# Weight stores of the first block issued by GpSimd instead of SyncE, in an AdaLN + 4-bit FFN kernel

## What is computed

```
gate = relu(cond @ W3 + b3)
z    = relu(((64 * x + sum_over_sequence(x)) * gate) @ W2 + b2)
w_up   = ((codes_up   - 7.5) * repeat(scale_up, 64)).T   + lora_a_up   @ lora_b_up
w_down = ((codes_down - 7.5) * repeat(scale_down, 64)).T + lora_a_down @ lora_b_down
out  = x + relu(z @ w_up + b_up) @ w_down + b_down
```

## Time and profile before

| | |
|---|---|
| median of 3 runs | 747.97 us (747.75 to 749.12) |
| the profiled execution | 748.49 us |
| its span, first to last instruction | 746.7 us |
| TensorE matmuls | 3274, busy 740.1 us (99%) |
| VectorE, ScalarE, GpSimd busy | 553.8, 419.9, 79.5 us |
| granted TensorE clock | 0.999 over the span |
| DMA | 170.20 MB, mean 228 GB/s |
| `made` store | 16 of 1280 KB, median 5.6 us to landing |
| `plain` store | 16 of 512 KB, median 8.2 us to landing |

### The profile page before, as it was taken

How to read it: one execution, slowest core, us unless ns; L and a number is a source line. 1 busy time by engine, 2 the same in 40 slices (tenths; PEclk the granted TensorE clock), 3 DMA queues, 4 the chain that set the end, 5 groups by cost and what they waited for, 6 DMA issues and landing times. The chain is left out here.

```text
span 746.7 us, 9586 instructions
## 1 busy us (share of the span) xinstructions
PE 740.1 (99%) x3274; PEld 613.2 (82%) x3274; DVE 553.8 (74%) x727; ACT 419.9 (56%) x727; POOL 79.5 (11%) x69
## 2 busy tenths in 40 slices
PE   9999999999999999999999999999999999999998
PEld 8888878878888878888888888888888888888886
DVE  6997776768948488767767687767775877757596
ACT  5963474766562565758456275666646353534540
POOL 0065524243420000000000000000000000000000
PEclk9999999999999999999999999999999999999999
DMA  9959968778444996666407896666515696666563
GB/s 291 322 178 378 319 228 280 253 250 274 169 197 141 376 331 222 212 195 194 161 27 252 284 382 225 226 198 197 184 57 193 221 386 223 189 190 195 196 194 130
DMA packets 68946, 170.20 MB, mean 228 GB/s; under 512 B 7650, under 2 KB 8034, under 8 KB 66338
## 3 DMA queue, kind: packets, MB, share of 16 engines
q1 hardware_dynamic: 68034, 168.20, 66.7%
q10 hardware_dynamic: 864, 1.39, 0.6%
HBM read 129.71 MB, written 40.89 MB: 228 GB/s over the span
## 5 line engine op out<-in xcount | busy, mean ns | idle before, releaser
L1186 PE MATMUL ps<-x_hi,ring 128*128 128x512 f32 x672 | 262.0, 390 | 0.6 <-issue 0.4
L1188 PE MATMUL ps<-x_hi,ring 128*128 128x512 f32 x672 | 261.8, 390 | 0.0
L1187 PE MATMUL ps<-x_lo,ring 128*128 128x512 f32 x672 | 261.7, 389 | 0.0
L1186 PEld LDWEIGHTS ps<-x_hi,ring 128*128 128x128 f32 x672 | 126.2, 188 | 27.8 <-ACT ps L526 1.0
L1188 PEld LDWEIGHTS ps<-x_hi,ring 128*128 128x128 f32 x672 | 126.2, 188 | 26.3
L1187 PEld LDWEIGHTS ps<-x_lo,ring 128*128 128x128 f32 x672 | 126.2, 188 | 26.0
L409 ACT ACTIVATE xt<-xt,gated,gate_n 128x64 f32<-128x64 f32 x216 | 74.7, 432 | 36.5 <-DVE gated L779 36.5
L518 ACT ACTIVATE f<-ps,small_in 128x512 f32<-128x512 f32 x96 | 64.8, 690 | 42.3 <-PE ps L1188 42.3
L971 DVE TENSOR_TENSOR x_lo<-x_sum,x_hi 128x512 fp32r<-128x512 f32 (+1 forms) x96 | 76.7, 819 | 4.2 <-ACT x_hi L556 3.4
L892 DVE TENSOR_TENSOR ps<-s,ps 128x512 f32<-128x512 f32 x48 | 33.3, 693 | 50.2 <-PE ps L1188 49.8
L929 DVE TENSOR_TENSOR res<-ps,res 128x512 f32<-128x512 f32 x71 | 47.6, 687 | 20.1 <-PE ps L1188 19.7
(11 more groups left out here) (90 smaller groups left out, 1024.4 us busy)
## 6 DMA issues: line engine op xcount, KB each, us to landing
ring<-made_w SPq DMA_DIRECT2D x336, 256.0 KB, 3.9
made_w<-made SPq DMA_DIRECT2D x16, 1280.0 KB, 5.6
xt<-in_x SPq DMA_DIRECT2D x32, 256.0 KB, 7.8
code<-in_codes SPq DMA_DIRECT2D x16, 512.0 KB, 8.4
scale<-made_s SPq DMA_DIRECT2D x16, 512.0 KB, 7.8
made_w<-plain SPq DMA_DIRECT2D x16, 512.0 KB, 8.2
res<-in_x SPq DMA_DIRECT2D x4, 2048.0 KB, 10.5
out<-res SPq DMA_DIRECT2D x12, 512.0 KB, 5.7
```

Of the source, the lines that this page charges most:

```text
L1186: pe.matmul(dest, w_hi, a_hi, start=start, stop=False, skip_group_check=True)
L1187: pe.matmul(dest, w_hi, a_lo, start=False, stop=False, skip_group_check=True)
L1188: return pe.matmul(dest, w_lo, a_hi, start=False, stop=stop, skip_group_check=True)
```

## The change

Both store functions move from SyncE's block to GpSimd's. GpSimd issues store_plain(u) and store_made(u) behind its four sums of unit u, with the same waits (L307, L312) and the same semaphores. SyncE's loop keeps scales, codes, the residual and the x tiles; its waits behind the loop stay.

```diff
@@ SyncE
-            def store_plain(u):
-
-                sp.wait_ge(plain_split, u + 1)
-                sp.dma_start(made_w[uid(FIRST[u]), :, 5:7],
-                             plain[u % 2][:, A11:A22 + 1].rearrange("p v h c -> p v (h c)").bitcast(F32)).then_inc(plain_stored[u % 2], 16)
-
-            def store_made(u):
-                sp.wait_ge(made_split, u + 1)
-                sp.dma_start(made_w[uid(FIRST[u]), :, 0:5],
-                             made[:, u % 2].rearrange("p c h v -> p c (h v)").bitcast(F32)).then_inc(made_stored[u % 2], 16)
...
-                store_plain(u)
                 if 2 <= u < 10:
                     load_x(1, u - 2)
-                store_made(u)
@@ GpSimd
+            def store_plain(u):
+
+                pool.wait_ge(plain_split, u + 1)
+                pool.dma_start(made_w[uid(FIRST[u]), :, 5:7],
+                             plain[u % 2][:, A11:A22 + 1].rearrange("p v h c -> p v (h c)").bitcast(F32)).then_inc(plain_stored[u % 2], 16)
+
+            def store_made(u):
+                pool.wait_ge(made_split, u + 1)
+                pool.dma_start(made_w[uid(FIRST[u]), :, 0:5],
+                             made[:, u % 2].rearrange("p c h v -> p c (h v)").bitcast(F32)).then_inc(made_stored[u % 2], 16)
...
                 pool.tensor_tensor(to[:, 4], w[:, A12], w[:, A22], ALU.subtract).then_inc(made_summed, 1)
+                store_plain(u)
+                store_made(u)
```

## The result

The changed kernel takes 762.1 us, median of 5 runs (761.85 to 762.9), against 747.75 (747.46 to 749.12) for the kernel before in the same comparison: a ratio of 1.0191 (95% interval 1.0179 to 1.0202), 14.35 us slower. The forecast was 9.1 us slower; direction and range hold, the size was more than a third too small. The profiled execution took 762.1 us with a span of 760.3, 13.6 us more than the profiled execution before (748.49 and 746.7).

The account below looks back on a forecast made before the run. TensorE, 99% busy, was taken as the bound, with VectorE just late for it in units 5 to 10. 7.1 + 2.0 = 9.1 us on 748.49 gave 757.6, less 0.5 for the median: 757.1 us, range 749 to 767.

Parts of the forecast that it names:

- the x2p_lo pair of unit 10: VectorE's two x2p_lo instructions before TensorE's unit 10 wait, delayed by GpSimd sums among them: 1.6 us.
- TensorE's wait in unit 10 ends later: Sum of VectorE's delays in units 5 to 9 and the x2p_lo pair, less 3.3 us of credits: +7.1 us.
- end of the stretch: Units 14 and 15: late sums(15) delay made_low(15), stalling TensorE 0.6 us, then a bank freed 1.4 us late: +2.0 us.
- The bound: TensorE is busy 99%; VectorE is just late with x2p_lo, so its delays in units 5 to 10 cost TensorE fully.
- The issue on GpSimd: Each store's DMA issue on GpSimd was taken as 1.1 us, between 0.32 and 1.71 us seen on SyncE.
- Rival (d): Slow GpSimd issue of 2 to 3 us, sums past made_high's place: 4 to 12 us more, 761 to 770; chance 0.22.
- The wait: GpSimd must await made_split(u) before sums(u+1), so they begin 1.1 us behind made_low(u), when VectorE is busiest.
- The step that failed: GpSimd's sums and VectorE's SBUF instructions alternate, each waiting for one instruction; 2.6 us each in units 5, 6, 9, 10.
- the credits: Gate and made_low no longer stand beside GpSimd: 2.0 and 1.3 us back over eight units, 3.3 us taken off.
- unit 7, a D unit: Sums run mostly beside VectorE's PSUM work, plain_low at 2.4 instead of 2.3, gate about 5.7 instead of 5.4: 0.3 us.
- Unit 4: Begins like unit 7 but with x2p_lo in it, 0.7 us; its made_low credit pays, so it ends no later.
- Stores as waits: Plain stores land by about when plain_high(u+2) wants them, counted 0; landing in 8 us would cost 1 to 2 us per unit pair.

Follow-up runs that it names:

- the wait alone: Kernel before, all stores on SyncE, plus one ordering: GpSimd starts the sums of unit u only when made_split has reached u; 750.65 us, ratio 1.0034.
- the small DMA in front of the sums: Kernel before (stores on SyncE) plus the made_split wait and a 2 KB GpSimd transfer between that wait and the sums; 765.48 us, ratio 1.023.
- the run with memsets: Changed kernel with GpSimd's four sums per unit replaced by memsets of the same outputs, so its output is wrong; 744.76 us, ratio 0.9956.
- the filled wait: Changed kernel with 16 extra matmuls ahead of TensorE's x2p_lo waits in units 6 and 10; 760.63 us, ratio 1.0167.
- the gap run: Changed kernel with a 64-column memset and a wait for it on GpSimd between the made store and the next sums; 756.68 us, ratio 1.0114.
- The runs with other orders: Changed kernel with store_made(u-1) issued after unit u's sums: behind the plain store 787.08 us; ahead of it, with an explicit made_split wait before the sums, 762.68 us.

## Why the prediction was right in sign and short in size

The ledger of TensorE, before against after, in the prediction's order. The forecast's figure is set beside what the traces show.

| | forecast | measured |
|---|---|---|
| made_low(9) ends later (155.80 to 164.27), from units 4 to 9 | +5.5 | +8.5 |
| the x2p_lo pair of unit 10 | +1.6 | +2.9 |
| TensorE's wait in unit 10 ends later (158.34 to 169.74) | +7.1 | +11.4 |
| from there to unit 15 (225.22 to 238.31), the 1.2 GHz stretch in it | none | +1.7 |
| end of the stretch (241.54 to 255.71 on TensorE) | +2.0 | +1.1 |
| behind it, where an old gap near 268 is gone | none | -0.6 |
| span | +9.1 | +13.6 |

*The bound.* Right for units 5 to 10: what makes VectorE later there is paid in full. But the ledger of the prediction began too late. TensorE waited 1.0 us for x2p_lo in unit 2 already, and was 1.6 us behind its old times at the start of unit 4's second half (LoRA matmuls at 88.19, before 86.64), 0.3 of it from before that wait.

*The issue on GpSimd.* Taken at 1.1 us between 0.32 and 1.71; measured 0.53 for made and 0.58 for plain. The 3.5 us of sums are uninterrupted, so in units 4 to 11 made_high never waits for GpSimd. Rival (d) is out by its own sign: the issue is fast. Its 761 to 770 us came to pass for another reason.

*The wait.* The prediction read one row wrongly: the 7.11 us of the earlier trace rows are how long GpSimd had been idle, while made_low(6), whose store it waited for, had ended at 119.94, 5.75 us before 125.69. Nothing in the sum rests on it. The step itself was right, and the first half of the cause: L742 begins directly behind made_low(u-1) and the issue, in VectorE's busiest time, and is waited for by no DMA. Its price with turns taken is what the wait alone shows, 2.6 us.

*The step that failed* is "Each waits until the other's instruction is over", taken as alternation: "GpSimd's 1.29, 0.73, 0.73 and 0.73 go between them". The row at 194.34 showed GpSimd holding VectorE for one sum, and that was read as one turn. In the changed kernel GpSimd holds it for four. The terms, as far as made_low(9), each with the credits (the shorter gate and made_low) added back: unit 7, a D unit, was put at 0.3 and cost 1.8, since plain_low is held for the rest of the sums (3.01 us for 1.23); unit 8, put at 0.7, cost 1.0; units 5, 6 and 9, put at 2.6 each, cost 2.2, 2.9 and 2.2. Behind them the x2p_lo pair was held 2.9 us instead of 1.6. The cost of units 5, 6 and 9 was thus about right for a wrong reason, which is luck, and that of the D unit and of the pair was 2.8 us too small in all.

The Trainium skill (SBUF — State Buffer, SBUF: two separate sides) says that whichever instruction starts first, GpSimd's or one of VectorE with two SBUF inputs, gets the port pair for the whole instruction. The wait alone agrees, turn by turn; the changed kernel goes beyond it: four sums run one behind the other for 3.4 us and hold one instruction of VectorE for 3.0, and the small DMA in front of the sums shows what makes the difference. The Trainium skill (SBUF — State Buffer, Who interferes with whom) also says that a GpSimd instruction which only writes SBUF doesn't contend with a two-input VectorE instruction; the run with memsets agrees, with x2p_lo at 689 ns.

*The clock* was missing from the sum. Behind the waits of 3.7 us TensorE came back at 1.2 GHz; behind the single 0.79 us of the earlier trace rows it hadn't. It costs some 1.5 us here, by the ledger and by the filled wait. The length of a wait alone doesn't tell whether it comes: see the gap run, where one of two waits of 2.42 us had no slow stretch behind it.

*Credits.* The lengths were right, gate 167 ns and made_low 1493, but the count was not. The 3.3 us are those of eight units, 4 to 11, and were taken off the cost of units 5 to 9. There they come to 2.4 us: 0.85 and 0.81 of gate in units 5 and 8, and 0.25 of made_low in each of units 6, 7 and 9. So 0.9 us too much was taken off.

*Unit 4.* Put at nothing; its made_low ends 0.7 us later (96.73 for 96.05). VectorE waits there for x2p_hi (2.03 us), and ScalarE, which makes it, waits 1.6 and 1.4 us for tiles of TensorE. So this is the wait of unit 2 coming back, and not GpSimd's work in unit 4. With the 0.9 us of credits and the 1.5 and 0.3 us of units 7 and 8, less 0.4 in units 5, 6 and 9 together, this makes the 3.0 us by which the table's first row is off.

*End of the stretch.* Sized at 0.6 and 1.4 us, measured as stalls of about 0.2 and 0.9: made_high(15) does wait for the sums and made_low(15) does end late (234.5, put at 222.0 plus the shift of some 11.4 to 13), but the first of the two stalls came out 0.4 and the second 0.5 us smaller than forecast.

*Stores as waits.* Next to nothing in this order, as forecast: ScalarE has one wait of 6.6 us for a plain store in the whole stretch, near 72 us (before, three of 16.3 us in all), and TensorE has no wait between 70 and 96. The runs with other orders show how near that was.

What stays open is why an issue lets GpSimd keep the port. Shown is only that a DMA issue directly in front does it, with 2 KB as with 1280, that a memset in front doesn't, that the sums of unit 0 with nothing in front aren't kept together either, and that a short memset with a wait behind the issue undoes it. How the remaining 5.4 to 6 us between the gap run and the wait alone divide into start offset and clock wasn't separated.

## What to carry to other kernels

Before a DMA issue is moved to GpSimd, look at what its wait drags along in program order, and at what VectorE reads from SBUF at that moment; the issue itself was the cheapest part of this change (0.53 us, hidden). If GpSimd must both issue and compute, keep the issue away from the front of its SBUF-reading instructions, and start these where VectorE is idle: here that ordering, with all stores on SyncE, took the kernel 1.4 us below the one before. If two stores share a queue, look at which of them is waited for first. Of a longer stall on TensorE, allow also for matmuls at half the clock behind it; here that was 1.5 us of 14.

## What was not expected of the hardware

- With a DMA issue directly in front, four GpSimd instructions ran for 3.4 us without a break and held one VectorE instruction with two SBUF inputs for 3.0 us of it; without the issue each side had its turn. Two sizes, 2 KB and 1280 KB, gave the same.
- After some waits TensorE ran 7 to 13 matmuls of 512 columns at 0.43 us from start to start instead of 0.23, and the length of the last wait doesn't decide it. It happened behind both waits of 3.7 us in the changed kernel, behind one of two waits of 2.42 us in the gap run, and behind 0.54 and 0.79 us close together with only the plain stores moved. It did not behind 0.51 and 1.49 us close together in the profiled execution of the wait alone (granted clock 1.000). Other executions of that same kernel differ: three of seven had 0.998 and took 751.7 to 752.1 us, four had 1.000 and took 749.6 to 750.7.
- An issue on GpSimd takes 0.53 to 0.58 us of the engine for 2 KB as for 1280 KB, between the 0.32 us for made and the 1.06 us for plain that SyncE showed.
- Behind another transfer on GpSimd's queue, a 1280 KB store went from 4.7 to 9.8 us to landing, and a 512 KB one from 5.5 to 9.3.
